# Eight-layer sequence kernel on one core: query and key parts stored once and gathered by six loads, maxima moved inside SBUF by GpSimd's queue, half the convolution matrix copied on chip

## What is computed

```
x = x + L0_attn(layernorm(x))   # projection, 3-tap conv, silu, a state space scan over time, gates, projection
x = x + L0_ffn(layernorm(x))    # experts that choose tokens, plus a shared expert
x = x + L1_attn(layernorm(x))   # linear attention
x = x + L1_ffn(layernorm(x))    # 2 of 8 experts for each token, plus a shared expert
x = x + L2_attn(layernorm(x))   # causal softmax attention, 16 heads of 8, low-rank q, k, v
x = x + L2_ffn(layernorm(x))    # linear, with routed low-rank parts
x = x + L3_attn(layernorm(x))   # leaky scan over time
x = x + L3_ffn(layernorm(x))    # softmax attention (16 heads of 8) and a hierarchical MoE, with norms
```

## Time and profile before

| | us |
|---|---|
| median of three runs | 3575.56 (3571.81 to 3576.92) |
| profiled execution | 3574.73 |
| its span | 3572.9 |

### The profile page before, as it was taken

How to read it: one execution, slowest core, us unless ns; L and a number is a source line. 1 busy time by engine, 2 the same in 40 slices (tenths; PEclk the granted TensorE clock), 3 DMA queues, 4 the chain that set the end, 5 groups by cost and what they waited for, 6 DMA issues and landing times. The chain is left out here.

```text
span 3572.9 us, 72294 instructions
## 1 busy us (share of the span) xinstructions
PE 2609.7 (73%) x20194; PEld 1892.7 (53%) x20194; DVE 2245.5 (63%) x4945; ACT 1580.3 (44%) x3615; POOL 634.1 (18%) x873
## 2 busy tenths in 40 slices
PE   3546749999987576998339999966565999973280
PEld 1333444459877433998226777756333555552270
DVE  5924966248777422776846666645885777765267
ACT  2503613334364233775235666632253667751253
POOL 0000100000000265554301111100120111102553
PEclk7878959999998687999679999968797999985585
DMA  3096100100091011222494565400097555510123
GB/s 94 7 258 176 53 0 18 35 18 0 0 156 54 20 46 43 70 69 89 152 276 62 71 73 71 57 1 1 0 293 109 69 68 75 71 43 19 53 77 100
DMA packets 335935, 263.34 MB, mean 74 GB/s; under 512 B 23132, under 2 KB 317452, under 8 KB 335308
## 3 DMA queue, kind: packets, MB, share of 16 engines
q1 hardware_dynamic: 314200, 227.03, 31.5%
q0 software_dynamic: 12928, 26.70, 2.2%
q10 hardware_dynamic: 8704, 8.39, 0.8%
HBM read 145.60 MB, written 114.86 MB: 73 GB/s over the span
## 5 line engine op out<-in xcount | busy, mean ns | idle before, releaser
L2444 ACT ACTIVATE h_pt<-h_ps 128x384 f32<-128x384 f32 (+1 forms) x1024 | 543.6, 545 | 306.2 <-PE h_ps L2353 151.8
L2197 DVE TENSOR_REDUCE h_nm<-h_ps 128x4 f32<-128x1024 f32 (+1 forms) x448 | 539.7, 1220 | 163.4 <-PE h_ps L2324 64.0
L1606 POOL DMA_INDIRECT sorted_rows<-e_row,e_pos x192 | 185.1, 964 | 443.4 <-DVE e_row L1585 239.6
L2372 PE MATMUL h_ps_o<-h_pt,h_vp 128*32 128x256 f32 (+1 forms) x4096 | 246.8, 358 | 1.3 <-ACT h_pt L2444 1.3
L1796 POOL DMA_INDIRECT results<-e_y,e_ykey x208 | 211.0, 1015 | 193.6 <-DVE e_y L1785 176.7
L1843 ACT ACTIVATE e_hid<-e_ps_h,e_wt 128x128 f32<-128x128 f32 x688 | 204.3, 369 | 27.7 <-PE e_ps_h L1817 19.0
L2358 PE MATMUL h_ps<-h_sq,h_sk 128*128 128x256 bf16 x1024 | 193.6, 275 | 23.9 <-DMA h_sq<-m_parts 13.6
L1817 PE MATMUL e_ps_h<-e_hT,e_wt 128*128 128x128 f32 x1376 | 201.9, 288 | 6.3 <-issue 2.6
L1825 PE MATMUL e_ps_o<-e_wt,e_hid 128*128 128x128 f32 x1376 | 198.0, 283 | 11.2 <-ACT e_hid L1843 10.4
L1753 DVE TENSOR_SCALAR e_wt<-w 128x1156 f32 (+1 forms) x208 | 140.0, 673 | 98.5 <-DVE e_y L1785 69.8
L1817 PEld LDWEIGHTS e_ps_h<-e_hT,e_wt 128*128 128x128 f32 x1376 | 179.7, 201 | 14.2 <-issue 10.4
(11 more groups left out here) (435 smaller groups left out, 6170.8 us busy)
## 6 DMA issues: line engine op xcount, KB each, us to landing
h_sq<-q_stack SPq DMA_DIRECT2D x64, 384.0 KB
h_sk<-k_stack SPq DMA_DIRECT2D x64, 384.0 KB
sorted_rows<-pad SPq DMA_DIRECT2D x26, 520.0 KB, 11.7
e_xt<-sorted_rows SPq DMA_DIRECT2D x104, 130.0 KB, 2.2
e_got<-results SPq DMA_DIRECT2D x24, 512.0 KB, 5.9
q_stack<-p_parts SPq DMA_DIRECT2D x32, 384.0 KB, 3.1
k_stack<-p_parts SPq DMA_DIRECT2D x32, 384.0 KB, 3.8
v_ones<-p_v SPq DMA_DIRECT2D x32, 288.0 KB, 2.7
```

What stands on the lines that cost most here:

```text
L1606: gp.indirect_dma_start(xs[:, :], bass.IndirectOffsetOnAxis(ap=pos[:, n % choices, tile:tile + 1], axis=0), row[n % ROWS][:, :], None).the ...
L2197: dve.tensor_reduce(to, got, AX, ALU.max, negate=True).then_inc(s["mx"].sem, 1)
L2372: ins = pe.matmul(ps_o[32 * j:32 * (j + 1), q0:], vp[u % 2][:, t, head(HG * g + j), :], pt[g % 2][:, j, t * SEQ:(t + 1) * SEQ - q0], start ...
L2444: act.activation(pt[g % 2][:, j, :], ps_2[:, h % 2, 0:SW], ACT.Exp, scale=scale).then_inc(s["ex"].sem, 1)
```

## The change

1. Convolution: `b_tz` becomes 64 columns wider, SP loads only rows 0 to 63 (two strips), and ACT (channels 0 to 3) and DVE (4 to 7) copy them, 64 columns on, to rows 64 to 127. The loops are written with `staggered`.
2. Collect with two choices: POOL adds the two results, DVE adds the sum to `x_res`; ACT clears the head buffers there; PE and DVE make the weight products there, with features reordered (feature-major instead of head-major).
3. Projection: the three parts of query and key are stored once each; the psum of query and key is tripled, the pipeline is deeper (lags 2 and 3); POOL takes the last subtraction of both in p2, of key in p3, and the memsets of `p_v`.
4. Attention: a batch's heads come by six loads, each query load followed by a key load that repeats one part 3, 2 and 1 times; the zeroing of rows 48 to 50 stays. POOL issues three DMAs from `h_mT` straight to rows 48, 49, 50 of `h_sq`, and its program is unrolled.

```
-                                for q in range(P // STRIP):
+                            for q in range(HALF // STRIP):
                                 late = P - (q + 1) * STRIP
                                 strip = bass.AP(rows.tensor, rows.offset + 1 + q * STRIP + late,
-                                                    [[1, STRIP], [P + SEQ, GC], [1, SEQ - late]])
+                                                [[1, STRIP], [P + SEQ, GC], [1, SEQ + HALF - late]])
+                    def lower_rows(j, q):
+                        return tz[j][HALF:P, 4 * q:4 * q + 4, 0:SEQ], tz[j][0:HALF, 4 * q:4 * q + 4, HALF:HALF + SEQ]
+                        def lower(n, j, r):        # on DVE; the same on ACT with half 0
+                            dve.wait_ge(*b_tz[j].now(r, 16 * (HALF // STRIP)))
+                            dve.tensor_copy(*lower_rows(j, 1)).then_inc(b_low[1].sem, 1)
+                        staggered(dve, UNITS, SLOTS, (0, stage), (0, lower), (1, kept))
+                        staggered(act, UNITS, SLOTS, (0, lower), (1, kept))
...
+                        @block.gpsimd
+                                    gp.wait_ge(*loads[j].now(i, 16 * choices))
+                                    gp.tensor_tensor(got[j][:, 0], got[j][:, 0], got[j][:, 1], ALU.add).then_inc(both[j].sem, 1)
+                            for rows in clear:
+                                act.activation(rows[:, :, :], none.unsqueeze(2).to_broadcast([P, NH, SEQ]), ACT.Copy
+                                               ).then_inc(cleared, 1)
...
-                        staggered(dve, NU, S, (0, normed), (2, split_on), (1, split))
+                        staggered(dve, NU, S, (3, values), (0, normed), (2, split))
+                        def last_part(n, j, r):
+                            for m in on_gp:
+                                gp.wait_ge(*s["mid"].now(n, m + 1))
+                                gp.tensor_tensor(parts[j][:, m, 2, :], rest[j][:, m, :], parts[j][:, m, 1, :],
+                                                 ALU.subtract).then_inc(s["lo_gp"].sem, 1)
-                        staggered(pe, NU, S, (1, project), (0, turn))
+                        staggered(pe, NU, S, (2, project), (1, turn), (2, project_v))
-                        staggered(act, NU, S, (1, first_part), (0, turned), (1, second_part))
+                        staggered(act, NU, S, (2, first_part), (1, turned), (2, second_part))
-                                sp.dma_start(to[0], parts[j][:, 0, 0:3 - i, :]).then_inc(s["stored"][j].sem, 16)
-                                sp.dma_start(to[1], parts[j][:, 1, i:i + 1, :].to_broadcast([P, 3 - i, U])
+                            for m, to in enumerate((q_parts, k_parts)):
+                                sp.dma_start(to.rearrange("a p t -> p a t")[:, :, ds(n * U, U)], parts[j][:, m, :, :]
...
-                                sp.dma_start(m_parts.rearrange("a h t -> (a h) t"), mT[:, :]).then_inc(s["mout"].sem, 16)
-                                sp.wait_ge(*at("mout", b + 1, 16))
-                                sp.dma_start(sq[ahead(u, r, 1)[0]][KR:KM, :, :], m_parts).then_inc(s["min"].sem, 16)
                                 spread_values(b + 1, *nxt)
+                                gp.wait_ge(*at("mc", b + 1, 1))
+                                for a in range(3):
+                                    gp.dma_start(sq[nxt[0]][KR + a:KR + a + 1, :, :], mT[a * NH:(a + 1) * NH, :]
+                                                 ).then_inc(maxima_in[tag], 16)
...
-            sp.dma_start(heads_in["sq"][u][0:KR, :, :], q_stack.rearrange("h e a t -> (e a) h t")[:, :, cols]).then_inc(up, 16)
-            sp.dma_start(heads_in["sk"][u][0:KR, :, :], k_stack.rearrange("h e a t -> (e a) h t")[:, :, cols]).then_inc(up, 16)
+            q_rows, k_rows = (d.rearrange("a (e h) t -> (a e) h t", h=NH) for d in (q_parts, k_parts))
+            row = 0
+            for i in range(3):
+                n = (3 - i) * HD
+                sp.dma_start(heads_in["sq"][u][row:row + n, :, :], q_rows[0:n, :, cols]).then_inc(up, 16)
+                part = k_rows[i * HD:(i + 1) * HD, :, cols]
+                again = bass.AP(part.tensor, part.offset, [[0, 3 - i]] + [list(d) for d in part.ap])
+                sp.dma_start(heads_in["sk"][u][row:row + n, :, :], again).then_inc(up, 16)
+                row += n
```

More of the change, by code:

```diff
@@ L2141, in run, with run_out, maxima_moved @@
                         step(b, b % SLOTS, b // SLOTS, first=b + 2 < NB, turn=b + 1 < NB, body=b < NB, tail=True)
+                def run_out(eng, step):
+                    for b in range(-2, NB + 1):
+                        step(b, b % SLOTS, b // SLOTS, first=b + 2 < NB, turn=-1 <= b < NB - 1, body=0 <= b < NB, tail=b >= 1)
+                def maxima_moved(eng, b):
+                    eng.wait_ge(maxima_in[tag], b * 48 + 48)
                 def ahead(u, r, n):
```

335 lines of the change are left out of this document (180 added, 155 removed).

## The result

The changed kernel takes **3767.49 us** (median of 4, 3765.11 to 3769.37), the kernel before, beside it, 3573.68 (3569.39 to 3576.92). The ratio is 1.0544, with a 95% interval of 1.0529 to 1.0559: 5.4% slower, where 62 us less was forecast. All that follows compares its profiled execution with that of before; the two spans are 3763.3 and 3572.9 us.

The account below looks back on a forecast made before the run. Bound by stage: transfers in convolution, transfers and closely DVE in projections, PE in attention. From 3574.7 us, -37 -3 -3 -25 -11 -12 -7 +31 -5 +10 = -62 gave 3513; own range 3480 to 3565, whole range 3465 to 3760.

Parts of the forecast that it names:

- rival 2: Attention's head loads: all 16 engines take part whatever the shape, so the 31 and 10 go; 3472 us, chance 0.12.
- the load's term: Attention steps: a batch's load takes 11.5 us against 11.4 available, just fits; 10 us added for scatter.
- My three rows for the price: Cost of a 512 B packet to an engine: 25.8 ns, 31.9 ns, and 69 ns in the crowded fill; 28 taken.
- Rival 1: Attention loads engine-bound at a dearer packet, 22.4 us per ns over 28; about 3600 us at 31.9 ns; chance 0.33.
- Initial fill: First head loads before each attention: 39.6 us against 24.1, so 15.5 more, twice, 31 us.
- Break-even: Packet price in attention's loads at which the whole gain of 62 us is gone: 30.8 ns.
- Maxima: Attention: moving the maxima to POOL's queue removes PE waits of 13.6 us in the second attention; -5 us taken.
- Convolution: Convolution: half the matrix copied on chip, 3.0 us a unit against about 4.15, 37 us less.
- Projections: Two projections: fewer stores and less DVE work, 25 us less in the first and 11 in the second, backlog apart.
- Collect, weights, clears: Collect: shared additions save 3 us, weight products under the first load save 3, moved clears count nothing.
- Backlog of stores: Between projection and first head load: the store queue ends sooner, 12 us less in the first, 7 in the second.
- Rival 3: Convolution and projections: POOL and DVE exclude each other, copies don't overlap; gains 18, 10 and 0, about 3559 us; chance 0.08.

Follow-up runs that it names:

- order 2, 0, 1: Changed kernel with parts stored once in order part 2, part 0, part 1, so each of six loads is 16 consecutive rows: 3418.45 us.
- runs of 16: Changed kernel with the six pairs of parts in another order, so every load is consecutive stored rows, seven loads and none repeating: 3551.46 us.
- key copies split: Changed kernel with each of the six 8-row key pieces loaded by a transfer of its own, ten transfers in place of seven: 3615.79 us.
- threefold split: Changed kernel with only the load making three copies of key part 0 split into three loads of 8 rows: 3707.62 us.
- the first three experiments: The runs key copies split, runs of 16 and threefold split, each against the changed kernel: 3615.79, 3551.46 and 3707.62 us.
- kernel stored six times: Changed kernel with query and key parts stored six times as before and read back by two loads of 48 rows: 3471.88 us.
- Six balanced loads in place of two: kernel stored six times, with each of its two 48-row loads made three loads of 16 rows: 3477.45 us.

## Why the prediction went wrong

**That the loads would be unevenly spread was right, and the trace counts it.** Each transfer ends in one small packet for each engine that it used. A batch of the changed kernel should have 12 + 16 + 8 of them from the query loads, 3 + 2 + 8 from the key loads, 3 from the clearing of the maxima rows, 16 from the values and 3 x 16 from GpSimd's three transfers: 116. One batch of the changed kernel (2152.2 to 2171.5 us) and one of the kernel with order 2, 0, 1 (2007.8 to 2021.7), where the sum is 6 x 16 + 3 + 16 + 48 = 163:

```profile
DMA packets 1959, 0.98 MB, mean 51 GB/s; under 512 B 116, under 2 KB 1956, under 8 KB 1956
```

```profile
DMA packets 2006, 0.98 MB, mean 71 GB/s; under 512 B 163, under 2 KB 2003, under 8 KB 2003
```

So rival 2 (all 16 engines whatever the shape) was rightly given little, and the number of engines of each transfer is as forecast. The trace doesn't name the engines, so that the transfers meet on the same first ones, which makes the 352, is not shown directly; the products below fit it.

**The step that failed is the price of a packet in the load's term, 1.6 + 352 x 0.028 = 11.5 us.** I took 28 ns and found that the load just fits its 11.4 us; it took 15.4 us. My three rows for the price were not on one measure: 31.9 ns came from the busy share of the queue, 25.8 and 69 from the time of 16 engines divided by the packets. The queue rows of these two stretches of the kernel before (2294.4 to 2295.0 and 1856 to 1876 us) give 28.4 and 87.5 ns by busy share. Nor was the cheap one a price with little in flight: all 16 engines were at work in it. Behind them stand a later stretch of the same load (2296 to 2298) and one of the changed kernel's step (2158.5 to 2159.5):

```profile
q1 hardware_dynamic: 372, 0.19, 110.1%
...
q1 hardware_dynamic: 4614, 2.36, 126.1%
...
q1 hardware_dynamic: 446, 0.22, 124.6%
...
q1 hardware_dynamic: 114, 0.06, 22.6%
```

The last two are 1.246 x 16 x 2000 / 446 = 89.4 ns with all engines at work, and 0.226 x 16 x 1000 / 114 = 31.7 ns with three or four. Over whole attentions, the queue row of the changed kernel's first one (1830 to 2410 us), that of the kernel before (1895 to 2335), and that of the kernel with order 2, 0, 1 (1810 to 2230):

```profile
q1 hardware_dynamic: 52164, 26.84, 19.5%
```

```profile
q1 hardware_dynamic: 53858, 28.37, 51.6%
```

```profile
q1 hardware_dynamic: 53480, 26.85, 59.2%
```

That is 0.195 x 16 x 580 / 52164 = 34.7 ns in the first, 67.4 in the second and 74.4 in the third. A packet's price is no constant. In the mean it rose from kernel to kernel as the load was spread over more engines, but the number of engines at work doesn't set it alone: in the kernel before, 16 engines at work paid 28.4 ns at 317 GB/s and 89.4 ns, at 112 GB/s, a microsecond later. The evenly spread loads run near 110 GB/s for most of their time (112 here, 118 in the fill), as if under a common limit; the changed kernel's load, 0.96 MB in 13.4 us, stays at 72 GB/s. The kernels also differ in how many rows a load writes, so what sets the price is open. With each kernel's own price, the packets on its busiest engine account for most of the transfers' time of a batch (first packet's start to last packet's end):

| kernel | busiest engine | ns each | product, us | transfers of a batch, us | steps, us |
|---|---|---|---|---|---|
| before | 112 | 67.4 | 7.5 | 7.6 | 14.2, 14.2 |
| order 2, 0, 1 | 112 | 74.4 | 8.3 | 8.9 | 13.9, 13.6 |
| runs of 16 | 144 | 73.5 | 10.6 | 10.9 | 15.7, 15.7 |
| key copies split | 176 | 60.5 | 10.6 | 11.5 | 16.5, 16.7 |
| threefold split | 272 | 45.3 | 12.3 | 12.6 | 17.8, 18.1 |
| changed kernel | 352 | 34.7 | 12.2 | 13.4 | 19.3, 18.9 |

This is also why the first three experiments gained less than they should: I took 39 ns from the changed kernel as fixed, and as the load was spread, the packets became dearer. In the two kernels with 112 packets on every engine the product is hardly more than an engine's busy time, so its fit says little; that of the four uneven ones says more. The steps grow a little more than the products. Rival 1 was the right mechanism: by its own scale (22.4 us for each ns over 28) 34.7 ns gives 3513 + 150 = 3663. The load took longer than its packets account for: read back through the term, (15.4 - 1.6) / 352 is 39 ns, which gives 3759. That this is so near to the measured 3767 is in part luck, since the scale leaves out the clock, and the stages outside the attentions gained 127 us where 98 were forecast. Two things come on top of the packets. One is SyncE: the third query load was issued in 4.12 us behind the two repeating loads (rows above), where a head load took 0.34 us in the kernel before, so the values' load behind it started late. The other is the clock, which lengthens the step and not the load: 1.3 us of the step above, about 40 us in each attention by PE's busy time (484 against 439 us in the earlier trace rows, and 464 against 425, for about as many matmuls). How much each is worth in the whole was not measured by itself.

**Initial fill:** the term failed in the same way, 26 and 29 us for 15.5 each; 50.1 us are 12.5 a batch.

**Break-even:** the time lies 7 us above the range, which ended at 39 ns for a packet and left out SyncE and the clock. I had written that the gain is gone at 30.8 ns, and that one of the two uncrowded rows lay above it. A range of 25.8 to 69 around a break-even of 30.8 spoke more for the loss than the 0.33 that I gave it; 28 was the price in the best 0.6 us of a load whose packets cost 67.4 ns in the mean over its attention.

**Maxima:** -5 forecast, -31 measured alone. The direction was right. I priced the edit by PE's recorded wait of 13.6 us and then cut it; the steps of a loop with PE bound (14.16 to 13.90, 14.18 to 13.54) showed more than the wait did.

**Convolution:** the mechanism was right and the size too small, 2.65 us a unit against 3.0 (84.9 / 32). The copies of the lower half, with the groups' columns as in the earlier trace rows:

```profile
L728 ACT ACTIVATE b_tz<-b_tz 64x1024 f32<-64x1024 f32 x30 | 31.6, 1055 | 37.5 <-DMA b_tz<-ktab 37.5
...
L696 DVE COPY b_tz<-b_tz 64x1024 f32<-64x1024 f32 x30 | 20.6, 687 | 27.4 <-DMA b_tz<-ktab 27.2
```

DVE's took 687 ns where I had scaled the 612 of 512 elements to 1.1 to 1.2 us. Both engines are idle before them for the strips, so the stage is bound by transfers still, at a DMA share of 1.10 and 270 GB/s.

**Projections:** -31 and -31 (backlog not counted in the first) for -25 and -18. The first came out near for a reason that was wrong in part, the second too small. I gave the gain to fewer stores and to DVE's relief together. The runs show that with six stores DVE's relief does nothing for the pace (5.42 us a unit, against 5.26 in the kernel before), and with two stores nothing that a measurement can tell (1.7 us). In the second projection it is the stores: with six of them it still took 100.8 us to the first head load, against 101.9 before and 70.7 in the changed kernel. In the first, 12.6 of the 31 us come without them. The kernel stored six times, from its first normalisation to its last copy of values:

```profile
1690.70 1.63 DVE L403 TENSOR_SCALAR p_nrm<-x_res,mean,rstd 128x128 f32<-128x128 f32 x6 [2.16 <-POOL p_v L2079]
...
1777.79 0.68 DVE L2064 COPY p_v<-p_ps_v 128x512 f32<-128x512 f32 x1
```

That is 87.1 us, against 99.7 before and 69.0 in the changed kernel. About half of the 12.6 lies at the start, where the cleared buffers are gone: from the first normalisation to the first subtraction it takes 5.9 us instead of 12.1. DVE sets the pace afterwards, busy 53.4 of 54 us.

**Collect, weights, clears:** -6, as forecast. **Backlog of stores:** -10 in the first for -12.

**Rival 3** (on-chip work takes the place of transfers) fell for the convolution, and was true in small for the projection's subtractions, where it cost nothing because it only cancelled itself.

## What to carry to other kernels

Price an unevenly spread transfer from both sides: count the packets on its busiest engine, and take the price (busy share x engines x time / packets) over whole loads in steady work, not over their best moment. Where the result is within a third of what the loop allows (here 11.5 us forecast became 15.4), look for an order of rows that spreads every load over all engines before making the change; here the same stored rows in another order turned 5.4% slower into 4.2% faster. A mean DMA share that falls while an engine waits for DMA is the sign to look for. Work moved from VectorE to GpSimd is a gain only after the lengthening of VectorE's other instructions has been subtracted.

## Seen of the hardware, and not expected

- The price of a packet of these loads (nearly all of 512 B), in the mean over an attention: 34.7 ns in the changed kernel, 45.3, 60.5 and 73.5 as the same bytes were spread over more engines, 74.4 with all 16 in six transfers. Within one load over 16 engines it went from 28.4 to 89.4 ns.
- A wait of PE of 2.75 us is followed by a stretch at a granted clock of 0.59 although PE is busy in all of it; over an attention the clock was 0.90 and 0.89, and PE's busy time for about as many matmuls 45 and 39 us longer. So in the step shown the late load costs about a third more than its lateness (4.0 + 1.3 us).
- In the steps, the third query load's issue on SyncE took 3.6 to 4.6 us behind transfers that use two and three engines; with all transfers over 16 engines it took about 0.6 to 0.7 (three query loads in 2.06 us). Few engines are not the only cause of a long issue: in the initial fills of the kernel before, whose head loads go over 16, one took up to 3.95 us.
- Six balanced loads in place of two cost 5.6 us in the whole kernel.
